# Orders of their own for the first and last rounds of a two-layer graph kernel, with VectorE written out and unread products of ones

## What is computed

```python
# layer 0 (X): attention, residual, normalisation
q, k, v = x @ Wq + bq, x @ Wk + bk, x @ Wv + bv          # 8 heads of 32
s = where(adj == 0, -inf, q k^T / sqrt(32)); p = softmax(s)
y = (p v) @ Wo + bo + x
y = layernorm(y) * gamma + beta
# layer 1 (Y): normalise, attention with a bias, residual, MLP
n = layernorm(y) * ln1_g + ln1_b
q, k, v = n @ wq + bq, ...
s = q k^T / sqrt(32) + where(adj > 0, 0.1 * adj * adj, -inf); p = softmax(s)
x1 = y + (p v) @ wo + bo
out = x1 + gelu(layernorm(x1)*ln2_g + ln2_b) @ w1 + b1) @ w2 + b2    # 256 -> 1024 -> 256
```

## Time and profile before

| | us |
|---|---|
| median of 3 runs (2091.73 to 2095.98) | 2095.86 |
| profiled execution | 2092.55 |
| its span | 2090.8 |
| TensorE busy | 2040.8 (98%) |
| ScalarE busy | 1649.2 (79%) |
| VectorE busy | 1598.8 (76%) |
| GpSimd busy | 1007.9 (48%) |

### The profile page before, as it was taken

The page is one execution under the profiler, slowest core; times in us unless marked ns, Lnnn a source line. Parts: engine busy times, 40 slices in busy tenths (PEclk is TensorE's granted clock), DMA queues, the critical chain, the costliest instruction groups (busy, mean ns, idle before and its releaser), DMA issues.

```text
span 2090.8 us, 59938 instructions
## 1 busy us (share of the span) xinstructions
PE 2040.8 (98%) x20032; PEld 1828.9 (87%) x20032; DVE 1598.8 (76%) x6911; ACT 1649.2 (79%) x5512; POOL 1007.9 (48%) x780
## 2 busy tenths in 40 slices
PE   6899999999999999999999999999999999999997
PEld 5689989889998889998889988889998889998886
DVE  5887877787877788777778777778777778777863
ACT  4688788878788878788888888887878887878863
POOL 3555445545445545445445445445455455455431
PEclk9999999999999999999999999999999999999999
DMA  4111100111100111100111100111100111101000
GB/s 139 32 32 42 42 27 16 40 40 40 40 18 22 40 40 40 40 11 29 40 40 40 40 10 30 40 40 40 40 10 30 40 40 40 37 13 31 27 11 21
DMA packets 80768, 72.80 MB, mean 35 GB/s; under 512 B 3009, under 2 KB 72257, under 8 KB 80705
## 3 DMA queue, kind: packets, MB, share of 16 engines
q1 hardware_dynamic: 80704, 71.98, 10.9%
HBM read 55.20 MB, written 16.78 MB: 34 GB/s over the span
## 4 chain that ended last, share of the span: by engine, by line
PE 94%; DVE 3%; ACT 2%; POOL 1%; issue 1%; DMA 0%; SPq 0%; ACTq 0%; DVEq 0%
PE ps L422 67%; PE ps L404 11%; PE ps L392 6%; PE ps L415 6%; PE ps L433 3%; ACT pm L539 1%; DVE pm L706 0%; DVE stats L780 0%; ACT hh L596 0%; DVE xy L795 0%; POOL y L890 0%; POOL y L895 0%; DMA pm<-in_wv 0%; ACT ps L597 0%; DVE actl L749 0%
## 5 line engine op out<-in xcount | busy, mean ns | idle before, releaser
L844 POOL TENSOR_TENSOR pm<-pm,rinv 128x512 f32<-128x512 f32 x512 | 520.8, 1041 | 604.8 <-DVE rinv L722 604.4
L539 ACT ACTIVATE pm<-pm,nmax 128x128 f32<-128x128 f32 x2048 | 792.7, 393 | 8.5 <-DVE nmax L706 8.1
L706 DVE CUSTOM_DVE_ANT_0 pm<-ps,m 128x128 f32<-128x128 f32 x2048 | 455.5, 285 | 38.5 <-PE ps L392 34.3
L539 ACT ACTIVATION_READ_ACCUMULATOR pm<-pm,nmax 128x1 f32 x2048 | 394.7, 193 | 0.0
L422 PE MATMUL ps<-w2h,hh 128*128 128x256 f32 x1024 | 295.6, 289 | 5.2 <-DVE hl L802 5.2
L404 PE MATMUL ps<-ident,pm 128*128 128x128 f32 x2048 | 290.7, 277 | 2.7 <-POOL pm L844 1.4
L422 PE MATMUL ps<-w2l,hh 128*128 128x256 f32 x1024 | 290.4, 284 | 0.0
L422 PE MATMUL ps<-w2h,hl 128*128 128x256 f32 x1024 | 290.4, 284 | 0.0
L863 POOL TENSOR_TENSOR rstd<-veps,power 128x4 f32<-128x4 f32 x96 | 97.3, 1014 | 370.4 <-DVE veps L788 370.3
L404 PEld LDWEIGHTS ps<-ident,pm 128*128 128x128 f32 x2048 | 230.7, 141 | 46.7 <-issue 19.5
L729 DVE COPY pt<-ps 128x512 f32<-128x512 f32 x256 | 176.0, 688 | 105.5 <-PE ps L404 105.4
(11 more groups left out here) (123 smaller groups left out, 5055.1 us busy)
## 6 DMA issues: line engine op xcount, KB each, us to landing
xTr<-in_xT SPq DMA_DIRECT2D x32, 512.0 KB, 4.6
xy<-in_x SPq DMA_DIRECT2D x32, 512.0 KB, 5.3
out<-x SPq DMA_DIRECT2D x32, 512.0 KB, 2.9
m<-in_adj SPq DMA_DIRECT2D x32, 256.0 KB, 2.8
a<-in_adj SPq DMA_DIRECT2D x32, 256.0 KB, 2.8
pt<-in_w SPq DMA_DIRECT2D x2, 512.0 KB, 8.8
pt<-in_w SPq DMA_DIRECT2D x1, 1024.0 KB, 12.0
r<-in_wo SPq DMA_DIRECT2D x2, 256.0 KB, 6.1
```

The costliest lines, as they stand in the source:

```text
L539: last = nc.scalar.activation(pm[:, g, h, :], pm[:, g, h, :], ACT.Exp, bias=nmax[:, g, h:h + 1], scale=-1.0, accum_out=rsum[:, g, h:h + 1])
L706: last = nc.vector.tensor_tensor_reduce(out=pm[:, g, h, :], in0=src[:, at:at + N], in1=m[:, g, :], scale=1.0, scalar=3e38, op0=ALU.add, op ...
L844: tt(pm[:, g, hs, :], pm[:, g, hs, :], rinv[:, g, hs].rearrange("p (h a) -> p h a", a=1).to_broadcast([P, HC, N]), ALU.mult).then_inc(norm ...
```

## The change

- `JOBS` loses the two BIAS jobs. `HEAD` and `TAIL` list, job by job and group by group, TensorE's order for rounds up to 4 and from 31 on; each engine has a `head()` and a `tail()` with orders of their own for the same steps. Counts are taken from `HEAD`, the loop and `TAIL` in turn.
- VectorE's 26 rounds between are written out instead of looped. Its body begins four calls later, and those four end the body before. The bodies of the other engines only lose the steps that exist for group 0 alone.
- TensorE makes 11 unread products of ones, 128x128x128, ahead of V0 0 of group 0 and 11 ahead of T1 0 of group 0, into the bank of the job that follows.
- wq, wk, wv of layer X have a semaphore each and are split one after the other; xT of group 0 and the columns are loaded by ScalarE's queue instead of SyncE's.
- The last group is stored in two halves, each behind its half of MLP2.

```diff
-FIRST, LAST = -1, NB - 1 + 3
-FIRST_FULL, LAST_FULL = 5, NB - 1 + FIRST
+FIRST_FULL, LAST_FULL = 5, NB - 2
+ONCE = {("BIAS", 0): 1, ("BIAS", 1): 1}
...
+        def iterate(eng, head, body, tail, written_out=False):
+            head()
+            if written_out:
+                for i in range(FIRST_FULL, LAST_FULL + 1):
+                    body(i)
+            else:
+                with eng.Fori(FIRST_FULL, LAST_FULL + 1) as i:
+                    body(i)
+            tail()
...
             def store(b):
+                if isinstance(b, int) and b == NB - 1:
+                    for j in (0, 1):
+                        taken(sp, b, "MLP2", j)
+                        gs = slice(2 * j, 2 * j + 2)
+                        sp.dma_start(o_b[b, :, gs, :], x1[:, gs, :]).then_inc(out_stored, 16)
...
+            def idle_products(b, name, n, times):
+                out = open_job(b, name, n)
+                for _ in range(times):
+                    mm(out[:, 0:P], ones[:, :], ones[:, :], start=True, stop=True)
...
+            def head():                                            # TensorE
+                qkv(X, 0, 0); qkv(X, 0, 1); qkv(X, 0, 2); qkv(X, 0, 3); scores(X, 0, 0); qkv(X, 0, 4); qkv(X, 0, 5)
+                scores(X, 0, 1); shift_products(0); flip(X, 0, 0, 0); flip(X, 0, 0, 1); flip(X, 0, 1, 0)
+                flip(X, 0, 1, 1); idle_products(0, "V0", 0, 11)
+                values(X, 0, 0); flip(X, 0, 2, 0); flip(X, 0, 2, 1); flip(X, 0, 3, 0)
+                flip(X, 0, 3, 1); out_proj(X, 0, 0); values(X, 0, 1); qkv(X, 1, 0); out_proj(X, 0, 1)
+                second_products(0); qkv(X, 1, 1); qkv(X, 1, 2); qkv(X, 1, 3); scores(X, 1, 0); qkv(X, 1, 4)
+                qkv(X, 1, 5); idle_products(0, "T1", 0, 11)
+                flip_rows("T1", 0, 0); flip_rows("T1", 0, 1); scores(X, 1, 1); flip(X, 1, 0, 0)
+                qkv(Y, 0, 0); qkv(Y, 0, 1); flip(X, 1, 0, 1); qkv(Y, 0, 2); qkv(Y, 0, 3); qkv(Y, 0, 4)
+                flip(X, 1, 1, 0); qkv(Y, 0, 5); scores(Y, 0, 0); flip(X, 1, 1, 1); flip(X, 1, 2, 0); flip(X, 1, 2, 1)
+                flip(X, 1, 3, 0); flip(X, 1, 3, 1); values(X, 1, 0); values(X, 1, 1); out_proj(X, 1, 0)
+                out_proj(X, 1, 1); flip(Y, 0, 0, 0); scores(Y, 0, 1); qkv(X, 2, 0); flip(Y, 0, 0, 1); qkv(X, 2, 1)
+                qkv(X, 2, 2); flip(Y, 0, 1, 0); flip(Y, 0, 1, 1); qkv(X, 2, 3); scores(X, 2, 0); values(Y, 0, 0)
...
+            def tail():                                            # TensorE, in part
...
+                out_proj(X, 31, 0); mlp_up(29, 3); values(X, 31, 1); mlp_up(29, 4); mlp_up(29, 5); out_proj(X, 31, 1)
+                mlp_up(29, 6); mlp_up(29, 7); flip(Y, 30, 0, 0); scores(Y, 30, 1); flip(Y, 30, 0, 1); mlp_down(29, 0)
...
+                qkv(Y, 31, 5); flip_rows("T2", 30, 0); scores(Y, 31, 0); flip_rows("T2", 30, 1); mlp_up(30, 0)
...
+                mlp_up(30, 7); flip(Y, 31, 0, 0); scores(Y, 31, 1); flip(Y, 31, 0, 1); mlp_down(30, 0)
...
+            def load_first():                                      # ScalarE
+                sc.dma_start(xTr[:, :, :], xT_v[:, :, 0:T]).then_inc(xT_loaded, 16)
+                sc.dma_start(par[:, :], w["columns"]).then_inc(cols_loaded, 16)
...
+            def head():                                            # ScalarE, in part
+                load_first(); before_first()
+                x_hi(0, 0); x_hi(0, 1); q_out(X, 0, 0); q_out(X, 0, 1); copy_wo(0); k_out(X, 0, 0); k_out(X, 0, 1)
+                exp(X, 0, 0, 0); exp(X, 0, 0, 1); exp(X, 0, 1, 0); exp(X, 0, 1, 1); exp(X, 0, 2, 0); exp(X, 0, 2, 1)
+                exp(X, 0, 3, 0); x_hi(1, 0); exp(X, 0, 3, 1); copy_pt(X, 0, 0); copy_pt(X, 0, 1); out_hi(X, 0, 0)
...
+                copy_pt(X, 1, 3); out_hi(X, 1, 0); out_hi(X, 1, 1); exp(Y, 0, 1, 0); exp(Y, 0, 1, 1); copy_pt(Y, 0, 0)
+                q_out(X, 2, 0); exp(Y, 0, 2, 0); q_out(X, 2, 1); k_out(X, 2, 0); exp(Y, 0, 2, 1); exp(Y, 0, 3, 0)
...
+            def split_part(n, by):                                 # VectorE
+                dve.wait_ge(part_loaded[n], 16)
+                cs = slice(n * D, (n + 1) * D)
+                split(wqkv_hi[0], wqkv_lo[0], C * n,
+                      [(wqkv[0][0][:, c, cs], wqkv[0][1][:, c, cs], raw_qkv[0][c][:, cs], by) for c in range(C)])
...
+            def head():                                            # VectorE, in part
+                split_q()
+                split_kv(0); x_lo(0, 0); x_lo(0, 1); mask0(0); mask_scores(X, 0, 0, 0); mask_scores(X, 0, 0, 1)
...
+                mask_scores(X, 0, 3, 0); mask_scores(X, 0, 3, 1); recip(X, 0, 2); shifts(0); x_lo(1, 0)
+                copy_pt(X, 0, 0); recip(X, 0, 3); copy_pt(X, 0, 1); out_lo(X, 0, 0); copy_pt(X, 0, 2)
+                copy_pt(X, 0, 3); x_lo(1, 1); split_qkv1(0, 0); out_lo(X, 0, 1); residual("WO0", 0, 0)
+                split_qkv1(0, 1); residual("WO0", 0, 1); norm_stats(0, 0); norm_rows(0, 0); mask0(1); second_shifts(0)
+                mask_scores(X, 1, 0, 0); norm_stats(1, 0); mask_scores(X, 1, 0, 1); mask_scores(X, 1, 1, 0)
+                norm_rows(1, 0); recip(X, 1, 0); v_out(X, 1, 0); mask_scores(X, 1, 1, 1); lo("T1", 0, 0)
...
+            iterate(dve, head, body, tail, written_out=True)
```

More of the change, by code:

```diff
@@ L41, with count_uses, uses_before @@
     ("F0", 0, 0, 2), ("WO1", 0, 2, 0), ("QKV1", 0, 1, 3), ("WO1", 1, 2, 1), ("QKV1", 1, 1, 2), ("F0", 1, 0, 0),
[7 rows of a table removed]
[6 rows of a table added]
 ]
+ONCE = {("BIAS", 0): 1, ("BIAS", 1): 1}
 BANKS = 8
-FIRST, LAST = -1, NB - 1 + 3
-FIRST_FULL, LAST_FULL = 5, NB - 1 + FIRST
+FIRST_FULL, LAST_FULL = 5, NB - 2
+HEAD = [
[37 rows of a table added]
+]
+TAIL = [
[19 rows of a table added]
+]
 def exists(b):
     return 0 <= b < NB if isinstance(b, int) else True
-POS = {(name, n): at for at, (name, n, _, _) in enumerate(JOBS)}
-BEHIND = [job[2] for job in JOBS]
-BANK = [job[3] for job in JOBS]
 def first(b):
     return isinstance(b, int) and b == 0
[L70 to L83, removed]
+BANK = {**{(name, n): bank for name, n, _, bank in JOBS}, **ONCE}
+BEHIND = {(name, n): behind for name, n, behind, _ in JOBS}
+PER_LOOP = [sum(bank == k for _, _, _, bank in JOBS) for k in range(BANKS)]
+def count_uses():
+    steady = [(name, n, i - behind) for i in range(FIRST_FULL, LAST_FULL + 1) for name, n, behind, _ in JOBS]
+    uses, before = [0] * BANKS, {}
+    for at, (name, n, b) in enumerate(HEAD + steady + TAIL):
+        before[name, n, b] = uses[BANK[name, n]], at
+        uses[BANK[name, n]] += 1
+    return before
+BEFORE = count_uses()
+def uses_before(b, name, n):
+    if isinstance(b, int):
+        return BEFORE[name, n, b][0]
+    behind, every = BEHIND[name, n], PER_LOOP[BANK[name, n]]
+    return (b + behind) * every + (BEFORE[name, n, FIRST_FULL - behind][0] - FIRST_FULL * every)
 def place(h):
@@ L233, in bank_of @@
         def bank_of(name, n):
-            return ps[BANK[POS[name, n]]]
+            return ps[BANK[name, n]]
         def free_of(name, n):
[L237 to L246, removed]
+            return job_free[BANK[name, n]]
+        def iterate(eng, head, body, tail, written_out=False):
[7 more added lines that the diff above has]
+            tail()
         def pt_slot(l, g):
@@ L269, in _, with load_xT @@
             o_b = w["out"].rearrange("(b g) t f -> b t g f", g=G)
-            xT_v = xT.rearrange("(c p) n -> p c n", p=P)
             def row(name):
                 return w[name].rearrange("(a n) -> a n", a=1).to_broadcast([P, D])
-            def load_xT(b, ahead=False):
-                if exists(b) and (ahead or not first(b)):
+            def load_xT(b):
+                if exists(b) and not first(b):
                     need(sp, act_hi[0], C * b)
@@ L449, in qkv @@
                 if exists(b):
[L450 to L451 removed]
+                    if first(b):
+                        pe.wait_ge(wqkv_lo[l], 2 * C if l else n // 2 * C + C)
                     if n == 0 and l == 0:
@@ L508, in _ @@
+            iterate(pe, head, body, tail)
         @block.scalar
@@ L614, in _ @@
+            iterate(sc, head, body, tail)
         @block.vector
@@ L805, in body @@
             def body(i):
-                mask_scores(Y, i - 2, 1, 0); out_lo(X, i - 1, 0); mask_scores(Y, i - 2, 1, 1); copy_pt(X, i - 1, 2)
-                copy_pt(X, i - 1, 3); split_qkv1(i - 1, 0); residual("WO0", i - 1, 0); recip(Y, i - 2, 0)
+                copy_pt(X, i - 1, 2); copy_pt(X, i - 1, 3); residual("WO0", i - 1, 0); recip(Y, i - 2, 0)
                 split_h(i - 3, 0); split_h(i - 3, 1); split_h(i - 3, 2); split_h(i - 3, 3); out_lo(X, i - 1, 1)
-                split_h(i - 3, 4); split_h(i - 3, 5); split_qkv1(i - 1, 1); split_h(i - 3, 6); x_lo(i, 0); x_lo(i, 1)
+                split_h(i - 3, 4); split_h(i - 3, 5); split_h(i - 3, 6); x_lo(i, 0); x_lo(i, 1)
@@ L820, in body @@
-                copy_pt(X, i, 0); norm_rows(2, i - 2); split_w1(i - 1, 1); recip(X, i, 2); shifts(i)
```

(6 more changed lines are left out.)

328 lines of the change are left out of this document (269 added, 59 removed), and 69 rows, old and new, of tables (HEAD, JOBS, TAIL).

## The result

The kernel after takes 2087.53 us in the median of 8 runs (2085.45 to 2087.91), the kernel before in the same rounds 2095.27 (8 runs, 2091.54 to 2096.98): a ratio of 0.9964, 95% interval [0.9953, 0.9974], so 7.7 us or 0.36% faster, where 2086 was forecast. The profiled execution of after took 2085.81, 6.7 less than that of before. The two differences are not the same because each profile is one of the faster runs of its kernel: those of before lie near 2092 (its profile; mean clock 0.993 in the runs beside the experiments) or at 2095 to 2098 (0.989 to 0.991), those of after at 2085.5 and 2085.8 (its profile) or at 2087.1 to 2087.9 (all 0.993 or more).

The account below looks back on a forecast made before the run. TensorE's own products bound each round at 62.97 us, so only filling and emptying could gain: 0.2 + 5.0 + 4.9 = 10.1 us less, 2082.4 for a profiled pass, 2085.8 as a median, said as 2086; range 2077 to 2093.

Parts of the forecast that it names:

- The loop, 0: The 26 rounds with VectorE written out: no change, bounds 0 and 1 us in a round.
- The start, -1.5: Up to TensorE's first product: 1.5 us gained by split weight loads, first product near 10.1, ends 0.7 and 2.3.
- wv then lands near 7.0: Step of the start: with xT loading beside the weights, wv lands near 7.0 us instead of 6.5.
- Until V, +1.5: Up to V of group 0: 2.4 lost to 11 ones less 0.9 back, 1.5 us lost, ends -0.3 and 2.4.
- a plain product of 128x256 takes 0.22 (four from 45.97 to 46.83), so 128 columns 0.11; 11 are 1.2 us: Cost of the ones ahead of V of group 0: 1.2 us at full clock, 2.4 at half.
- 0.9 for V: Time given back ahead of group 0's later work because V may run at full clock: 0.9 us.
- Until T1, -0.2: Up to T1 of group 0: 0.2 us gained, T1 near 65.9 instead of 66.09, ends -2 and 3.
- The second 11 products lie beside those 1.4 us: 0, or 1.0: Ones ahead of T1 of group 0 run beside 1.4 us for the rows: cost 0, or 1.0 at half clock.
- 66 to 117, -5.0: Filling from 66 to 117 us: 5.0 us gained as layer Y's exponentials start earlier, ends 1 and 9.
- S(X,2,0) near 100.4: Sign for the filling: group 2's scores start near 100.4 us instead of 105.88.
- The emptying, -4.9: Last rounds: 4.9 us gained up to mlp_down(29), mlp_down(30) and by the last store in halves, ends 1 and 8.
- The rivals: Chains hold the filling, 2092, chance 0.17; new orders fit wholly, 2076, 0.14; slower through VectorE's long straight program, 2112, 0.07.

Follow-up runs that it names:

- e8: The changed kernel with VectorE's rounds 5 to 30 in a hardware loop again, nothing else; 2087.31 us, ratio 0.9964.
- the four last experiments: e9 to e12: the changed kernel with x on SyncE's queue behind the weights, 22 products of ones ahead of the last T2; 2077.43 to 2080.85 us.
- e7: The changed kernel with xT and columns of group 0 on SyncE's queue behind the weights, and the last group stored in one piece; 2087.95 us.
- e9: The changed kernel without ones in the filling, 22 ahead of the last T2, x on SyncE's queue behind the weights; 2080.85 us.
- e3: The changed kernel without the second set of ones, ahead of T1 of group 0; 2085.45 us, ratio 0.9949.
- e11: e10 plus 5 products of ones ahead of V of group 0, in the free bank of F0 5; 2077.43 us, ratio 0.9916.
- e1: The changed kernel without both sets of products of ones; 2084.46 us, ratio 0.9943.
- e10: e9 plus 11 products of ones ahead of T1 of group 0, in the free bank of S0 7 of group 1; 2079.94 us.
- e4: The changed kernel with its tail undone: rounds 31 to 34 run through the old body on every engine; 2090.27 us, ratio 0.9974.
- e12: e11 with the first bias products, moved behind the first four flips, in place of the 5 ones ahead of V; 2080.85 us, ratio 0.9926.
- e5: The changed kernel with V's ones cut to 5 in F0 5's bank, T1's 11 in the bank of S0 4 of group 1; 2087.67 us.
- e2: The changed kernel without the first set of ones, ahead of V of group 0; 2084.28 us, ratio 0.9944.
- e6: e5 plus 22 products of ones in the wait ahead of T2 of the last group; 2084.54 us, ratio 0.9955.

## Why the prediction came out as it did

**The number and the sum.** The sum was 10.1 us for a pass like the profiled one, 2082.4; that pass took 2085.81, so the sum was 3.4 too large. The median forecast missed by 1.5 alone, mostly because I added 3.3 for the distance between the profile and the median of before, and in after that distance is 1.7. Half of the error was covered by the other, which is luck. And 3.4 is the error of the sum at its mildest: after's profile is one of the two fastest of its eight runs, and e8's, with the same work on TensorE, is 2.1 us longer.

**The loop, 0: right.** 1763.10 us from round 3 to round 31 against 1763.25, and e8.

**The start, -1.5: wrong.** The first product stood at 11.06, not near 10.1, and the first scores 0.2 later than before. The step that failed is "wv then lands near 7.0", with nothing said of wq and wk. In after wq landed 4.5 us from its issue, against 2.8 to 3.0 in the four last experiments, where x comes behind it; wk began its sweep at 6.76, and the other two sweeps and the small steps then ran without a gap to 9.6. With wq and wk both late, a semaphore for each part let only the first sweep run ahead. The Trainium skill (DMA: Bandwidth & Descriptors, "Queues, rings and completion order") has every DMA engine serve the queues in turn, a packet from each; the two landing times agree with it. I had used that page for its sum of bandwidth and not for who goes first: a transfer on a second queue does not wait behind the weights, it takes its share from them. With x behind the weights instead, VectorE's sweeps were over by 8.0 in e7 and 7.8 in e9, and it then waited 1.1 and 1.8 us for the high part of x: there x is what comes last.

**Until V, +1.5: wrong in one term.** The place was right: the ones ran behind the wait, V right behind them, and the event that released them was copy_pt's. The chain without them was right too (16.23 against 16.19). The term "a plain product of 128x256 takes 0.22 (four from 45.97 to 46.83), so 128 columns 0.11; 11 are 1.2 us" was mis-sized. The kernel issues each of these f32 products as two instructions, as it already did in the rows I quoted: L373 is called twice and has x4, L376 has x32 for 16 calls. Eleven are 22, 0.1 us each at full clock and 0.2 at half, and they took 4.51 us at a mean clock of 0.56, against an upper end of 2.4 (windows of after, both sets):

```profile
36.39:40.90 4.51, 4.51 (x23) 4.39 (x23) 0.00 (x0) 0.12 (x1) 3.82 (x3) 0.56 0.00 0
...
66.79:70.92 4.13, 4.13 (x22) 4.13 (x23) 2.75 (x14) 2.33 (x13) 2.04 (x2) 0.60 0.01 2
```

What they give back was too small as well: 0.9 for V. V and its flips gave 1.4, and the half-clock stretch behind the second bias products was 1.6 us shorter in e3 and e11 than in e1, e9 and e10. Of that stretch the prediction said "what they do to the clock stays: no change"; it cost 0, 1.6 or 3.2 in these profiles, and why is open.

By the Trainium skill (FP8 and Floating Point Precision, "TensorE Precision Notes") a true FP32 product makes four passes through the array. The trace agrees: at full clock 11 of these products of 128 columns take 2.62 us in e11, 0.24 each, which is what a product of 512 columns in the rounded format takes (48 of the last mlp_up in 11.18 us, 0.23 each). That the kernel issues two instructions for each is read from the trace alone.

**Until T1, -0.2: wrong by the same term.** T1 came 30.02 us behind V (before 29.97), and V was 4.8 later. "The second 11 products lie beside those 1.4 us: 0, or 1.0" failed: the bank's mask step was done 1.24 us before the rows, and the products took 4.13, so 2.9 stood on the path. I had taken full clock there because it was 1.00 in before; there the wait was 1.72 us, and here it was 2.05 and the clock 0.60.

**66 to 117, -5.0: right.** From T1 to the scores of group 2 4.6 were won (3.1 in e4, e7 and e8, where the clock fell at the flips of group 1), to round 3 another 1.2; the idle 9.8 us of that stretch fell to 5.35, from T1 to 117. The sign that I named, S(X,2,0) near 100.4, failed by 5.7 us, at 106.09: 5.0 of it is T1, at 70.92 instead of 65.9.

**The emptying, -4.9: right in size, with luck in the pass.** 5.65 were won in after's profile, and it would be 4.0 with the fall at mlp_up(30,0) that eight of twelve profiles have: the distance from round 31 to mlp_down(29) fell from 65.0 to 63.0 us and the clock stayed at 1.00 there, that to mlp_down(30) from 114.3 to 109.8, and the store in halves gave 0.8 where 0.4 was taken. The chain behind the last V kept its waits (5.57, 1.50 and 2.15 us).

**The rivals.** None of them came; what came is a case that I did not have: the new orders won 11.6 us behind T1, and ahead of it 4.8 were lost, 4.5 of them between the first scores and V, to the ones. The bounds of the two sets, 2.4 and 1.0, should have held that case; both were drawn from a count of 11 instructions.

## What to carry to other kernels

Unread products that keep the clock up pay only if they end before the wait does: give them a bank that is free when the wait begins, since in the follower's bank they start when the wait is over, and take their number from the instructions in the trace, not from the calls. Placed so, 5 and 11 of them gained 4.2 us from the first scores to those of group 2 in the profiles, 3.4 in the medians (e9 to e11), where 11 and 11 behind the waits had cost 3.1 in the same stretch (e1 to after). When a step is worth its warm clock, count also what stands behind it until the next wait. And before a stretch of one profile is called a gain, look at the same stretch in other profiles with the same code: here four places differed by 1.5 us or more between them.

## What the runs showed of the hardware

- Bias products for 3.9 us, all but the first 0.9 us of one column, left V at half clock (e12: 1.94 us for 32 instructions, against 1.08), as an idle wait of 3.8 us did (e1).
- The clock can fall while TensorE has no idle time: in and behind the second bias products the mean clock was 1.00, 0.85 or 0.73 over the same products (e5, e11, e10).
- The same instructions behind the same idle 2.25 us ran at full clock in after, e2, e3 and e6 and took 1.6 us longer in the eight others; behind 1.82 us the clock fell in five profiles of thirteen, behind 2.15 us in two of fourteen. The same head took 16.24 us to a V at full clock in e5 and 16.23 to one at half in e6.
- Two VectorE instructions of 128x128 took 0.48 us near 7.5 us (e7), 1.66 us at 32 us (e11) and 3.20 us at 36 us, while GpSimd worked (e12).
- The first 256 KB load landed in 4.2 to 4.6 us instead of 2.8 to 3.0 when a 512 KB load was issued at the same time on another engine's queue (eight profiles against six).
